# LoRA-A of gate and up inside the last feature tile, and that tile third in the opening

## The reference, cut to what matters

```python
def lora_add(base, inp, A, B):            # H = 512, F = 1376, RANK = 16
    Ab, Bb = A[layer_idx][lora_indices], B[layer_idx][lora_indices]
    t = jnp.einsum('bri,bni->bnr', Ab, inp)            # LoRA-A
    return base + jnp.einsum('bor,bnr->bno', Bb, t) * SCALE   # LoRA-B
gate = lora_add(jnp.einsum('bnh,fh->bnf', x, W_gate), x, A_gate, B_gate)
up = lora_add(jnp.einsum('bnh,fh->bnf', x, W_up), x, A_up, B_up)
act = jax.nn.silu(gate) * up
down = lora_add(jnp.einsum('bnf,hf->bnh', act, W_down), act, A_down, B_down)
```

## Time and profile before

| | |
|---|---|
| median of 3 executions | 361.28 us (361.18 to 361.67) |
| profiled execution: its time / its span | 359.89 us / 358.2 us |
| TensorE busy | 354.3 us, 99% of the span, 1728 matmuls |
| VectorE busy | 197.6 us, 55% |
| ScalarE busy | 141.2 us, 39% |
| GpSimd busy | 83.2 us, 23% |
| DMA | 38.86 MB, mean 108 GB/s |
| granted TensorE clock, mean | 1.000 |

### The profile page before, as it was taken

How to read it: one execution, slowest core, us unless ns; L and a number is a source line. 1 busy time by engine, 2 the same in 40 slices (tenths; PEclk the granted TensorE clock), 3 DMA queues, 4 the chain that set the end, 5 groups by cost and what they waited for, 6 DMA issues and landing times.

```text
span 358.2 us, 4760 instructions
## 1 busy us (share of the span) xinstructions
PE 354.3 (99%) x1728; PEld 299.2 (84%) x1728; DVE 197.6 (55%) x303; ACT 141.2 (39%) x191; POOL 83.2 (23%) x89
## 2 busy tenths in 40 slices
PE   8999999999999999999999999999999999999996
PEld 7888888888888888988888898888888888888886
DVE  3758664245434533576574476769888868511101
ACT  5567444234423432434662552547363353201100
POOL 1738886644240001100000000000032054002200
PEclk9999999999999999999999999999999999999999
DMA  7855542333130041579317209201042012101011
GB/s 253 274 167 168 176 133 62 113 102 88 53 108 0 0 171 47 164 276 345 96 48 214 93 2 354 116 5 53 3 158 77 2 59 73 47 29 59 31 59 59
DMA packets 14979, 38.86 MB, mean 108 GB/s; under 512 B 2305, under 2 KB 4097, under 8 KB 13681
## 3 DMA queue, kind: packets, MB, share of 16 engines
q1 hardware_dynamic: 11728, 31.24, 25.8%
q0 software_dynamic: 2656, 6.95, 6.6%
q10 hardware_dynamic: 576, 0.43, 0.4%
HBM read 36.51 MB, written 2.10 MB: 108 GB/s over the span
## 4 chain that ended last, share of the span: by engine, by line
PE 99%; DVE 0%; issue 0%
PE ps L1052 28%; PE ps L1053 28%; PE ps L1054 28%; PE ps L1174 3%; PE ps L1072 3%; PE ps L1080 1%; PE ps L1087 1%; PE ps L1103 1%; PE ps L1091 1%; PE ps L1095 1%; PE ps L1264 1%; PE ps L1251 1%; PE ps L1273 0%; PE ps L1282 0%; DVE x L1045 0%; DVE warm L746 0%
## 5 line engine op out<-in xcount | busy, mean ns | idle before, releaser
L1052 PE MATMUL ps<-x_hl,w_hl 128*128 128x512 f32 x160 | 62.8, 392 | 0.0
L1053 PE MATMUL ps<-x_hl,w_hl 128*128 128x512 f32 x160 | 62.7, 392 | 0.0
L1054 PE MATMUL ps<-x_hl,w_hl 128*128 128x512 f32 x160 | 62.3, 389 | 0.0
L383 POOL DMA_INDIRECT b_raw<-b_gu,row_of x36 | 36.1, 1003 | 34.7 <-DVE b_st L713 25.4
L421 POOL TENSOR_TENSOR am_hl<-am_raw,am_hl 128x512 fp32r<-128x512 f32 x8 | 11.1, 1392 | 136.8 <-ACT am_hl L438 136.8
L734 DVE TENSOR_TENSOR glu<-glu,ps 128x512 f32<-128x512 f32 x22 | 15.0, 685 | 37.6 <-PE ps L1072 37.6
L1054 PEld LDWEIGHTS ps<-x_hl,w_hl 128*128 128x128 f32 x160 | 30.1, 188 | 6.5
L438 ACT ACTIVATE act<-glu 128x512 f32 (+1 forms) x22 | 13.8, 632 | 54.3 <-DVE glu L734 54.2
L1052 PEld LDWEIGHTS ps<-x_hl,w_hl 128*128 128x128 f32 x160 | 30.1, 188 | 5.2
L1053 PEld LDWEIGHTS ps<-x_hl,w_hl 128*128 128x128 f32 x160 | 30.2, 189 | 4.8
L1053 PE MATMUL ps<-act,wd_hl 128*128 128x512 f32 x80 | 31.1, 389 | 0.0
(11 more groups left out here) (139 smaller groups left out, 700.6 us busy)
## 6 DMA issues: line engine op xcount, KB each, us to landing
wc_raw<-mask_w SPq DMA_DIRECT2D x8, 1024.0 KB, 7.4
w_raw<-w_gu SPq DMA_DIRECT2D x9, 512.0 KB, 3.4
wd_raw<-w_dn SPq DMA_DIRECT2D x10, 256.0 KB, 3.0
x_raw<-x_t SPq DMA_DIRECT2D x8, 256.0 KB, 5.3
w_raw<-w_t SPq DMA_DIRECT2D x2, 1024.0 KB, 6.9
x<-x_t SPq DMA_DIRECT2D x2, 1024.0 KB, 6.1
am_raw<-a_moe SPq DMA_DIRECT2D x8, 256.0 KB, 2.7
bm_raw<-b_moe SPq DMA_DIRECT2D x4, 512.0 KB, 3.8
```

Of the source, the lines that this page charges most:

```text
L383: nc.gpsimd.indirect_dma_start(b_raw[f % 2][:, p].rearrange("q m f -> q (m f)"), None, b_gu, bass.IndirectOffsetOnAxis(ap=row_of[:, f - 2, ...
L1052: nc.tensor.matmul(out, w_high, m_high, start=start, stop=False)
L1053: nc.tensor.matmul(out, w_high, m_low, start=False, stop=False)
L1054: return nc.tensor.matmul(out, w_low, m_high, start=False, stop=stop)
```

## The change

The 32 columns of the last feature tile that were zeros now hold the LoRA-A factors of gate and of up for the two sequences of a pair. As those factors are different for each pair, there are four versions of the tile's weights (`w_last`, one for each `p`), and the tile is made by pairs: 256 columns a matmul, 4 pairs x 2 matrices x 4 `k` x 3 = 96 matmuls (`project_last`), in place of 48 of 512 columns. The 32 matmuls of `lora_down` and the stationary tile `a_st` are gone. LoRA-A's result comes out in partitions 96 to 127 of the tile's banks.

The last tile goes third in the opening: first half of tiles 0 and 1; `project_last(0)`; second half of tile 0; LoRA-B of three first halves (12 matmuls); `project_last(1)`; second half of tile 1; LoRA-B of three second halves (12 matmuls); then tiles 2 to 9. Six half tiles are taken out of PSUM in the opening, in the order of `FIRST_EVICTED`, where there were four.

The loads change place too: SP loads the last tile's weights ahead of the second half of `x`, then the factors of five sequences, then the second half of `x`; POOL loads LoRA-B's factors of the first two pairs (of three tiles) ahead of its LoRA-A factors. `load_ad` waits until the last tile's second half has been made. LoRA-B's factors take 96 partitions in place of 128, and their low part is one operation of 32 x 1024 in place of two of 32 x 512.

```diff
+LAST = FT - 1
+FIRST_EVICTED = ((0, 0), (1, 0), (LAST, 0), (LAST, 1), (0, 1), (1, 1))
+FIRST_BANK = (4, 0, 2, 4, 6, 0)
```

SyncE's queue:

```diff
-            for k in range(KD):
-                sp.dma_start(x_raw[:, k, HALF:T], x_t[:, k, HALF:T]).then_inc(dma_x1[k], 16)
+            sp.dma_start(w_last_raw[:], w_gu[LAST]).then_inc(dma_w_last, 16)
             sp.wait_ge(dma_small, 16)
             for b in range(A_BY_SP):
...
+            for k in range(KD):
+                sp.dma_start(x_raw[:, k, HALF:T], x_t[:, k, HALF:T]).then_inc(dma_x1[k], 16)
             sp.dma_start(const_sb[:], consts).then_inc(dma_const, 16)
```

GpSimd's queue:

```diff
-            load_b_first()
-            for f in range(2, FT):
-                pool.wait_ge(b_hi, f - 1)
-                pool.wait_ge(b_lo, 2 * f - 2)
+            load_b_first(0)
+            for b in range(A_BY_SP, BATCH):
...
+            load_b_first(1)
+            for f in range(2, LAST):
+                if f < 4:
+                    pool.wait_ge(bf_lo, 3 * f - 3)
+                else:
+                    pool.wait_ge(b_hi, f - 3)
+                    pool.wait_ge(b_lo, f - 3)
                 load_b(f)
                 if f == AD_LOADS_AFTER:
+                    pool.wait_ge(up_ready, evicted(LAST, 1) + 1)
                     load_ad()
```

ScalarE's queue:

```diff
             def b_high(f, slot, use):
                 act_e.wait_ge(dma_b[slot], 16 * NPAIR * (use - 1))
                 if isinstance(f, int) and f == 2:
-                    act_e.wait_ge(up_ready, 3)
-                copy(b_st[slot][:], b_raw[slot][:]).then_inc(b_hi, 1)
+                    act_e.wait_ge(up_ready, evicted(0, 1) + 1)
+                copy(b_st[slot][0:F_LAST], b_raw[slot][0:F_LAST]).then_inc(b_hi, 1)
...
+            for p in range(2):
+                w_last_high(p)
+            a_high(0)
+            for k in range(KD):
                 x_high(k, 1)
...
+            b_first_high(0)
+            for p in range(2, NPAIR):
+                w_last_high(p)
+            a_high(1)
             t_high(0)
+            b_first_high(1)
+            first_silu(0)
+            first_silu(1)
+            first_act_high(0)
+            first_act_high(1)
+            first_silu(2)
+            first_act_high(2)
             w_high(2, 0, 2)
             t_high(1)
-            for u in range(2):
-                act_high(u, u, u, 0)
-            act_e.wait_ge(act_lo, 1)
-            silu(2, 0, 2)
+            for n in range(3, 5):
+                first_silu(n)
+                first_act_high(n)
             b_high(2, 0, 2)
-            act_e.wait_ge(act_lo, 2)
-            silu(3, 1, 6)
+            first_silu(5)
+            first_act_high(5)
```

VectorE's queue:

```diff
+            for p in range(2):
+                w_last_low(p, p + 1)
+            a_low(0, 3)
+            for k in range(KD):
                 x_low(k, 1)
...
             b_first_low(0)
+            for p in range(2, NPAIR):
+                w_last_low(p, p + 3)
+            a_low(1, 7)
             dve.wait_ge(dma_const, 16)
...
             t_mask(0)
+            t_low(0)
             b_first_low(1)
+            first_gate(0)
+            first_gate(1)
+            first_act_low(0)
+            first_act_low(1)
+            first_gate(2)
+            first_act_low(2)
             w_low(2, 0)
             t_mask(1)
             t_low(1)
+            for n in range(3, 5):
+                first_gate(n)
+                first_act_low(n)
             b_low(2, 0)
+            first_gate(5)
+            first_act_low(5)
```

TensorE's queue:

```diff
+            def project_last(s):
+                bank = FIRST_BANK[2 + s]
+                pe.wait_ge(wl_hi, 4 * s + 4)
+                pe.wait_ge(wl_lo, 4 * s + 4)
+                for m in range(2):
+                    if s == 1:
+                        pe.wait_ge(glu_done if m else silu_done, 1)
+                    for p in (2 * s, 2 * s + 1):
+                        cols = slice(p * PAIR, p * PAIR + PAIR)
+                        for k in range(KD):
+                            last = mm3(ps[:, bank + m, PAIR * (p % 2):PAIR * (p % 2) + PAIR],
+                                       w_last[:, p, 0, k, m], w_last[:, p, 1, k, m],
+                                       x_hl[:, 0, k, cols], x_hl[:, 1, k, cols],
+                                       k == 0 and p % 2 == 0, k == KD - 1 and p % 2 == 1)
                 last.then_inc(t_ready, 1)
...
-            for p in range(2):
-                lora_down(p)
+            project_last(0)
             for k in range(KD):
                 for m in range(2):
...
             last.then_inc(w0_used, 1)
-            for p in range(2, NPAIR):
-                lora_down(p)
-            adapt_first(0)
+            pe.wait_ge(t_hi, 2)
+            pe.wait_ge(t_lo, 1)
+            pe.wait_ge(bf_hi, 3)
+            pe.wait_ge(bf_lo, 3)
+            for n in range(3):
+                adapt_first(n)
+            project_last(1)
             for m in range(2):
-                pe.wait_ge(t_masked, m + 1)
-                project(1, 1, m, 1)
-            adapt_first(1)
+                pe.wait_ge(glu_done if m else silu_done, 2)
+                project(1, FIRST_BANK[5] + m, 1)
+            pe.wait_ge(t_hi, 4)
+            pe.wait_ge(t_lo, 2)
+            pe.wait_ge(bf_hi, 6)
+            pe.wait_ge(bf_lo, 6)
+            for n in range(3, 6):
+                adapt_first(n)
...
+            def tile_half(f, u, s):
+                bank = 4 * (1 - u) + 2 * s
+                pe.wait_ge(silu_done, 2 * f + s)
+                project(u, bank, s)
                 if s == 0:
-                    pe.wait_ge(b_hi, f + 1)
-                    pe.wait_ge(b_lo, 2 * f + 2)
+                    pe.wait_ge(b_hi, f - 1)
+                    pe.wait_ge(b_lo, f - 1)
```

More of the change, by code:

```diff
@@ L115, in slots @@
         def slots(name, shape, dtype, offset):
-            return [at(f"{name}{u}", shape, dtype, R_U + 20 * KB * u + offset) for u in range(2)]
+            return [at(f"{name}{u}", shape, dtype, R_U + 20 * KB * (1 - u) + offset) for u in range(2)]
         x_hl = at("x_hl", [P, 2, KD, T], F32R, R_X)
@@ L513, in t_high @@
                 act_e.wait_ge(t_masked, g + 1)
[L515 to L518, removed]
[L520 to L522 removed]
+                for rows in (slice(0, 32), slice(64, 96)):
+                    copy(t_st[rows, two], t_raw[0:32, two]).then_inc(t_hi, 1)
+            b_first_high(0)
+            for p in range(2, NPAIR):
+                w_last_high(p)
+            a_high(1)
+            t_high(0)
+            b_first_high(1)
[5 more added lines that the diff above has]
+            first_act_high(2)
             w_high(2, 0, 2)
[L524 to L525 removed]
             t_high(1)
[L527 to L530 removed]
+            for n in range(3, 5):
+                first_silu(n)
+                first_act_high(n)
             b_high(2, 0, 2)
[L532 to L536 removed]
+            first_silu(5)
+            first_act_high(5)
+            with act_e.Fori(0, (FT - 5) // 2) as i:
                 for u in range(2):
@@ L541, in _ @@
                     evacuate(2 * i + 2 + u, u)
+            w_high(FT - 2, 1, FT // 2)
+            b_high(FT - 2, 1, FT // 2)
+            evacuate(FT - 3, 0)
             act_e.wait_ge(up_ready, 2 * FT - 2)
@@ L761, in _, with w_last_low @@
             x_low(3, 0)
-            for k in range(2):
-                x_low(k, 1)
[L764 to L774, removed]
+            def w_last_low(p, n):
+                dve.wait_ge(wl_hi, n)
+                low(w_last_own(p, 1), w_last_raw[:, :, :, 0:F_LAST], w_last_own(p, 0)).then_inc(wl_lo, 1)
@@ new lines, in a_low, with b_first_low @@
+            def a_low(g, n):
+                for par in range(2):
+                    dve.wait_ge(wl_hi, n + par)
+                    low(a_part(1, g, par), a_own(g, par), a_part(0, g, par)).then_inc(wl_lo, 1)
+            for p in range(2):
+                w_last_low(p, p + 1)
+            a_low(0, 3)
+            for k in range(KD):
+                x_low(k, 1)
+            def b_first_low(g):
+                two, rows = slice(2 * g, 2 * g + 2), slice(64, 96)
+                for u, stack in enumerate((b_st[0], b_st[1], b_last)):
+                    dve.wait_ge(bf_hi, 3 * g + u + 1)
+                    low(stack[rows, two], b_first[rows, two, u], stack[rows, two]).then_inc(bf_lo, 1)
@@ L801, in _ @@
             b_low(2, 0)
-            gate(3, 1, 7)
-            for u in range(2):
-                act_low(2 + u, u, u, 1)
-            with dve.Fori(0, (FT - 3) // 2) as i:
+            first_gate(5)
+            first_act_low(5)
+            with dve.Fori(0, (FT - 5) // 2) as i:
                 for u in range(2):
@@ L809, in _ @@
                     evacuate(2 * i + 2 + u, u)
+            w_low(FT - 2, 1)
+            b_low(FT - 2, 1)
+            evacuate(FT - 3, 0)
             dve.wait_ge(dma_lora, 32)
@@ L1057, in halves, with project @@
                 return slice(s * HALF, s * HALF + HALF)
-            def project(slot, bank, m, s, first=False, part=range(KD)):
```

(21 more changed lines are left out.)

228 lines of the change are left out of this document (120 added, 108 removed).

## The result

The changed kernel takes 365.7 us (median of 4, 364.68 to 365.85) against 361.32 (median of 4): ratio 1.0112, 95% interval 1.0094 to 1.0130. It is 1.1% slower; forecast was 360.7, in a range of 359.6 to 362.0. Its profiled execution took 364.68 us with a span of 363.0, 4.8 us more than the span shown before.

What follows compares the result with a forecast made beforehand. TensorE, busy 99% of the span, was taken as the bound: -3.3 us saved, +2.6 wait for LoRA-B's factors of tile 2, +0.1 handovers, so the median goes from 361.28 to 360.7 us, range 359.6 to 362.0.

Steps and rivals of the forecast that it cites:

- (b): Opening, `t_st` needed at 27.90: x's last load lands at 16.9, ready 9.7 us later; cost nothing, bound 0.8 us.
- What TensorE saves: TensorE's matmuls: `lora_down` and one tile removed, `project_last` added; 3.3 us less, bounds 3.3 to 4.0.
- the rival in which the split costs nothing: Last tile: two matmuls of 256 columns take what one of 512 does; saving 3.8, time 360.2 us; chance 2%.
- (a): Opening, `project_last(0)` at 16.69: weights there before 11.3, factors ready by about 15; in time by 1.5 us.
- (c): Opening, `t_st` for the second LoRA-B group at 40.56: ready at 39.1, in time by 0.5 us or more.
- LoRA-B's factors of tile 2: Start of tile 2: two whole half tiles stand ahead of these splits on ScalarE and VectorE; TensorE waits 2.6 us.
- The clock: Rival, behind tile 2's 2.6 us gap: TensorE's clock falls to 1.2 GHz, +2.7 to +5.5 us, 363.4 to 366; chance 6%.

Runs made afterwards that it cites:

- run 3: Changed kernel with LoRA-B's factors of tile 2 split right behind silu(3) and gate(3), and GpSimd's last 590 KB held until x landed: 356.97 us, ratio 0.9886.
- run 1: Changed kernel with LoRA-B's factors of tile 2 split right behind silu(3) and gate(3), ahead of the rest of two half tiles: 360.98 us, ratio 0.9990.
- run 2: Changed kernel with GpSimd holding LoRA-B's factors of the last two pairs (590 KB) until the second half of x landed: 361.23 us, ratio 0.9989.
- run 4: Changed kernel with SyncE issuing the second half of x right behind the last tile's weights, ahead of the LoRA-A factors: 366.02 us, ratio 1.0127.

## Why the prediction was wrong

Two terms that the sum had at nothing failed: the wait for `t_st` at the end of the opening (b), which cost 2.8 us, and the fall of the clock behind a long gap, 1.5 us. Against the 0.6 us less that were forecast, either alone was enough to make the kernel slower.

- *What TensorE saves: right.* 3.3 us forecast; 3.25 us in the trace of run 3, where no wait hides it. The pace of 0.12 us for 256 columns held, with 96 rows too. The upper bound was worked out wrong: with 0.114 in every term the saving is 3.7 and not 4.0, and the rival in which the split costs nothing mixes the two paces (3.6 to 3.7 and not 3.8).
- *(a) The last tile's first half: the margin was wrong.* Cost nothing was forecast, with 1.5 us to spare. The raw weights landed at 11.8 (by 11.3 was forecast), the LoRA-A factors at about 16, and their splits were over at 17.3 and not by 15. The part began at 17.43. Only 0.15 us of that shows as a later start than TensorE's own, since TensorE was 0.6 us late by then, from its first matmuls ahead of 8 us; on time, it would have waited for the factors. Both vary: delays of 0.3 to 0.4 us ahead of 8 us are in two of three profiles of the kernel before, and in run 1, with the same loads, the factors landed at 15.1 and the part began at 16.70. How much of the 0.7 us belongs to the change is open.
- *(b) `t_st` at 27.90: this step failed.* The chain behind the landing was right: L + 9.7 with L = 21.4 gives 31.1, and TensorE resumed at 31.00. L was mis-sized: 16.9 forecast, bound 19.0, measured 21.4. I took the long landings of the opening for those of a full queue and the engines as free behind it. In fact the engines stayed full to 20 us, at 260 to 275 GB/s, with GpSimd's factor loads beside those of `x`. Run 2 shows that these loads are the cause: without the last 590 KB of them `x` landed 3.8 us earlier. It cost 2.3 + 0.5 us where 0 was forecast and 0.8 was the bound.
- *(c) `t_st` at A: right*, no wait.
- *LoRA-B's factors of tile 2: right.* 2.6 us forecast, 48.53 to 51.15 measured; 2.6 in runs 2 and 4 too, which kept the order.
- *The clock: the rival came true*, with the place and the sign that I gave it, at a chance of 6% that was far too low. The sum took the clock at full level behind the gap, with no row for it, as the prediction itself said. Its price, +2.7 to +5.5, was too high: six matmuls ran at the lower level and not 12 or more, and the fall costs 1.5 us in the trace, 1.3 and 1.6 in runs 1 and 2. It was said to decide the sign from 1.4 us on; against 0.6 us less it does so from 0.6 us on, and 1.5 came. In the timed executions the mean clock was 0.991 in three of four, 1.1 us longer than the profiled one with 0.995. A second fall would fit that, but no trace shows one, and run 1 has an execution at 0.991 with a single long gap.
- *The base.* The sum was made on a profile that lacked about 1.2 us of waits that the two other profiles of the kernel before have. So the saving on the median is larger than 3.3: run 3 is 4.26 us below before, which is 3.25 and the 1.0 us wait that goes too.

Put together: -3.3 - 1.0 + 2.8 + 2.6 + 2.6 (1.5 and 1.1 for the two steps of the clock) = 3.7 against 4.4 measured on the medians. The 0.7 us that are left are as large as the late start in the profiled execution; that the others have it too is not shown. Left open: the held-back silu in the kernel before, what brings the mean clock of some executions to 0.991, and what makes the full engines slow beside GpSimd's loads: their indirect kind, small packets, or the mixture. Packets under 2 KB alone don't explain it (15 to 20 us).

## What to carry to other kernels

When a stage is put into a hand-written order, look at what now stands ahead of each operation that had a small margin, on each engine; here a margin of 0.24 us decided 2.6 us, and moving one operation in two queues gave it back. Loads that are moved ahead take the engines from those behind: count the bytes between two deadlines at the rate that such traffic reaches in the trace, 260 GB/s here and not 374. A gap of TensorE of 2.5 us cost up to 1.6 us more than its length here, one of 0.5 us did not.

## What the runs showed of the hardware that was not expected

- Full DMA engines (share 1.09 to 1.10) moved only 232 to 283 GB/s from 10 to 16 us, with GpSimd's factor loads among the traffic, and 374 GB/s from 5 to 10 us; in run 2, with GpSimd's queue idle from 14 to 16 us, it was 373.
- In run 2 the mean clock was 0.995 in six of ten executions with the same gap of 2.5 us and 1.000 in the other four; the times lie 1.6 us apart, and the one with a trace shows the clock at 0.52 to 0.63 for the 4 us behind the gap. In one trace a gap of 2.5 us brought the clock down and one of 2.3 us did not (changed kernel), in another one of 4.3 us did and one of 2.5 us did not (run 4). A gap of 0.5 us never did it in four executions.
- Two matmuls of 256 columns take 0.24 us, one of 512 takes 0.228: 12 ns for the split.
